# A recommender kernel: SyncE fetches the rows of 7 of its 416 gathers one by one, and rows are buffered for four tiles

## What is computed

```python
e = jnp.stack([tbl_0[ids[:, 0]], ..., tbl_25[ids[:, 25]]], axis=1)
x = layer_norm(dense_t @ Wd.T, gd, bd)
y = layer_norm(jnp.einsum('bnd,ed->bne', sparse_t, Ws), gs, bs)
y = layer_norm(jnp.einsum('bne,pn->bep', y, Wsi), gsi, bsi)
T = jnp.concatenate([x[:, None, :], jnp.swapaxes(y, 1, 2)], axis=1)
Z = jnp.einsum('bnd,bmd->bnm', T, T)
out = layer_norm(Z[:, TRIL_I, TRIL_J] @ Wl.T, gl, bl) * mask
h = jnp.maximum(jnp.concatenate([z, r_dense_t], axis=1) @ W_top1 + b_top1, 0.0)
h = jnp.maximum(h @ W_top2 + b_top2, 0.0)
y = h @ W_top3
```

## Time and profile before

| what | value |
|---|---|
| median of 3 runs | 592.68 us (590.53 to 594.43) |
| the profiled execution | 590.05 us |
| its span, first to last instruction | 588.3 us |
| mean granted TensorE clock | 0.962 |
| busy PE, PEld, DVE, ACT, POOL | 87%, 67%, 68%, 48%, 69% |
| instructions | 17016 |

### The profile page before, as it was taken

How to read it: one execution, slowest core, us unless ns; L and a number is a source line. 1 busy time by engine, 2 the same in 40 slices (tenths; PEclk the granted TensorE clock), 3 DMA queues, 4 the chain that set the end, 5 groups by cost and what they waited for, 6 DMA issues and landing times.

```text
span 588.3 us, 17016 instructions
## 1 busy us (share of the span) xinstructions
PE 511.5 (87%) x6783; PEld 396.6 (67%) x6783; DVE 402.2 (68%) x707; ACT 283.7 (48%) x727; POOL 406.5 (69%) x421
## 2 busy tenths in 40 slices
PE   2768768999999999999999988898899888998785
PEld 1654447678777777878787667676677666676564
DVE  2746766887878787787877766777577766777500
ACT  0513553545555464646464545454364545454422
POOL 6777777777777777777777777777777777773000
PEclk9958887999999999999999999999899999999999
DMA  7711113131313131313131312213131312212010
GB/s 266 270 27 28 25 29 87 27 89 28 88 29 87 30 88 28 90 29 87 29 91 26 88 28 67 50 36 81 28 88 28 88 28 66 50 30 75 2 62 2
DMA packets 27198, 36.39 MB, mean 62 GB/s; under 512 B 8917, under 2 KB 17775, under 8 KB 26607
## 3 DMA queue, kind: packets, MB, share of 16 engines
q0 software_dynamic: 13312, 13.66, 12.8%
q1 hardware_dynamic: 13808, 21.65, 10.9%
HBM read 26.09 MB, written 9.18 MB: 60 GB/s over the span
## 4 chain that ended last, share of the span: by engine, by line
PE 30%; DVE 22%; issue 16%; POOL 16%; ACT 8%; DMA 7%; SPq 1%; DVEq 0%; ACTq 0%
POOL rows L512 16%; PE bank_z L634 8%; DVE y L391 4%; PE bank_z L671 4%; DVE y_var L401 4%; DMA rows<-in_table,ids_all 4%; DVE r_vec L416 4%; PE bank_z L621 3%; PE bank_b L608 3%; PE bank_a L598 3%; DVE scaled L356 2%; ACT y_sq L761 2%; PE bank_z L587 2%; DVE y_r L408 2%; DMA wsi_b<-in_wsi_b 2%
## 5 line engine op out<-in xcount | busy, mean ns | idle before, releaser
L512 POOL DMA_INDIRECT rows<-in_table,ids_all x416 | 405.3, 974 | 126.8 <-issue 121.9
L401 DVE TENSOR_REDUCE y_var<-y_sq 128x32 f32<-128x1024 f32 x64 | 78.1, 1220 | 45.3 <-ACT y_sq L761 45.3
L761 ACT ACTIVATE y_sq<-y 128x512 f32<-128x512 f32 x128 | 80.4, 631 | 38.4 <-DVE y L391 38.0
L621 PEld LDWEIGHTS bank_z<-r_vec 128*32 128x32 f32 x4096 | 47.8, 112 | 60.6 <-issue 59.2
L608 PE MATMUL bank_b<-mixed,gs_row 64*128 64x512 f32 x128 | 74.7, 664 | 15.6 <-ACT mixed L790 15.4
L598 PE MATMUL bank_a<-wsi_b,scaled 128*128 128x192 f32 (+3 forms) x512 | 84.5, 309 | 2.1 <-DVE scaled L381 2.0
L416 DVE TENSOR_TENSOR r_vec<-y,y_r 128x512 f32<-128x512 f32 x128 | 82.9, 689 | 2.2
L598 PEld LDWEIGHTS bank_a<-wsi_b,scaled 128*128 128x128 f32 x512 | 78.5, 196 | 3.6 <-DVE scaled L381 3.2
L634 PE MATMUL bank_z<-wl,zd 128*128 128x512 f32 x160 | 77.7, 616 | 0.6 <-DMA zd<-zx 0.6
L608 PE MATMUL bank_c<-mixed,gs_row 64*128 64x512 f32 x128 | 74.7, 664 | 0.0
L783 ACT ACTIVATE row_std<-row_var,eps 128x8 f32<-128x8 f32 (+1 forms) x64 | 19.2, 300 | 103.8 <-DVE row_var L365 74.5
(11 more groups left out here) (99 smaller groups left out, 624.5 us busy)
## 6 DMA issues: line engine op xcount, KB each, us to landing
zx<-zs SPq DMA_DIRECT2D x16, 560.0 KB, 3.6
rows<-in_table,ids_all POOLq DMA_INDIRECT x416
dense_t<-in_dense_t SPq DMA_DIRECT2D x1, 2048.0 KB, 8.5
wl<-in_wl SPq DMA_DIRECT2D x1, 1280.0 KB
w<-in_w SPq DMA_DIRECT2D x1, 1280.0 KB, 16.2
zd<-zx SPq DMA_DIRECT2D x16, 80.0 KB
wsi_b<-in_wsi_b SPq DMA_DIRECT2D x1, 1248.0 KB, 11.6
zd<-zx SPq DMA_DIRECT2D x16, 70.0 KB
```

Of the source, the lines that this page charges most:

```text
L401: v.tensor_reduce(y_var[:, k % BANKS, :], y_sq[:, k % 2, :, :].rearrange("e a (s p) -> e (a s) p", p=PROJ), AX_X, ALU.add).then_inc(y_var_ ...
L512: nc.gpsimd.indirect_dma_start(rows[t % 2][:, c, D * blk:D * (blk + 1)], None, io["table"], bass.IndirectOffsetOnAxis(ap=ids_all[:, n:n + ...
L621: mm = pe.matmul(bank_i[PROJ * s:PROJ * (s + 1), n * ITEMS:(n + 1) * ITEMS], own[:, Y0:PAD], own, start=True, stop=True)
L761: nc.scalar.activation(y_sq[:, k % 2, blk, :], y[:, k % 2, blk, :], ACT.Square).then_inc(y_squared, 1)
```

## The change

One half of one chunk (chunk 12, half 1: the last gather of a tile) is no longer gathered by POOL in seven tiles: 1, 4, 6, 8, 11, 13 and 15. SP fetches those 7 x 128 rows instead. The ids of these rows are loaded as two small tensors (`sp_ids`, `sp_base`), added on DVE, and read by SP into registers, eight at a time (`TENSOR_LOAD`). For each row SP then computes the address from a register (listed as `ISA` below) and issues one DMA of one row into one partition of `rows`. The first 128 rows (tile 1) are fetched after the loads; after that each pass of SP's loop fetches 56 rows: 8 between the `zx` DMA and the wait for it, and 48 after the seven `zd` DMAs. Loop 13 has 40 rows left, loops 14 and 15 none. `rows` has four buffers instead of two, used in turn by tile, with semaphores to match; before the first row of a tile from 4 on, SP waits until the rows of the tile four before are scaled. PE waits, in the last quarter of these seven tiles, also for SP's 128 rows.

```diff
+SP_CHUNK, SP_BLK = CHUNKS - 1, 1
+SP_TILES = [1, 4, 6, 8, 11, 13, 15]
+SP_BATCH = 8
+SP_EARLY = 1
+SP_SHARE = 56
+BUFFERS = 4
...
+def by_sp(t, c, blk):
+    return t in SP_TILES and (c, blk) == (SP_CHUNK, SP_BLK)
+
+
+def gather_count(t, q):
+
+    return sum(not by_sp(i, c, blk) for i in range(t % BUFFERS, t + 1, BUFFERS) for c in GROUPS[q] for blk in range(2))
...
-        rows = [sb(f"rows{i}", [P, CHUNKS, 2 * D]) for i in range(2)]
+        rows = [sb(f"rows{i}", [P, CHUNKS, 2 * D]) for i in range(BUFFERS)]
...
             step(v.memset(ones[:], 1.0), "constants")
+            dve.wait_ge(sp_ids_loaded, 32)
+            v.tensor_tensor(sp_ids[:], sp_ids[:], sp_base[:], ALU.add).then_inc(sp_ids_ready, 1)
...
             for dst, src in ((ids_all, "ids"), (row_base, "row_base")):
                 sp.dma_start(dst[:], io[src]).then_inc(s_ids, 16)
+            for dst, src in ((sp_ids, "sp_ids"), (sp_base, "sp_base")):
+                sp.dma_start(dst[:], io[src]).then_inc(sp_ids_loaded, 16)
...
+            def fetch(first, end):
+
+                for at in range(first, end, SP_BATCH):
+                    u, p0 = divmod(at, P)
+                    t = SP_TILES[u]
+                    if p0 == 0 and t >= BUFFERS:
+                        sp.wait_ge(rows_scaled, BANKS * (t - BUFFERS + 1))
+                    _, found = nc.values_load_multi_w_load_instructions(
+                        sp_ids[u:u + 1, p0:p0 + SP_BATCH], engines=(mybir.EngineType.SP,), min_val=0,
+                        max_val=io["table"].shape[0] - 1, skip_runtime_bounds_check_because="ids are rows of the tables")
+                    for n, row in enumerate(found):
+                        p = p0 + n
+                        sp.dma_start(rows[t % BUFFERS][p:p + 1, SP_CHUNK, D * SP_BLK:D * (SP_BLK + 1)],
+                                     io["table"][bass.ds(row, 1), :]).then_inc(sp_rows[u], 16)
+
+            sp.wait_ge(sp_ids_ready, 1)
+            fetch(0, SP_EARLY * P)
             sp.wait_ge(prep, prep_at["zd"])
             for t in range(TILES):
...
                 sp.dma_start(zx.rearrange("j p k g i -> (j p) k g i"), zs[:]).then_inc(z_out, 16)
+                done = [min(SP_EARLY * P + n, len(SP_TILES) * P)
+                        for n in (SP_SHARE * t, SP_SHARE * t + SP_BATCH, SP_SHARE * (t + 1))]
+                fetch(done[0], done[1])
                 sp.wait_ge(z_out, Z_OUT * (t + 1))
...
+                fetch(done[1], done[2])
...
-                if t >= 2:
-                    pool.wait_ge(rows_scaled, k - 2 * BANKS + 1)
+                if t >= BUFFERS:
+                    pool.wait_ge(rows_scaled, k - BUFFERS * BANKS + 1)
                 for c in GROUPS[q]:
                     for blk in range(2):
+                        if by_sp(t, c, blk):
+                            continue
...
-                pe.wait_ge(gathered[t % 2][q], (t // 2 + 1) * (32 * len(GROUPS[q])))
+                pe.wait_ge(gathered[t % BUFFERS][q], 16 * gather_count(t, q))
+                if t in SP_TILES and q == BANKS - 1:
+                    pe.wait_ge(sp_rows[SP_TILES.index(t)], 16 * P)
```

More of the change, by code:

```diff
@@ L115, in tower @@
         row_base = sb("row_base", [P, 2 * CHUNKS], I32)
+        sp_ids = sb("sp_ids", [len(SP_TILES), P], I32)
+        sp_base = sb("sp_base", [len(SP_TILES), P], I32)
         ws_t = sb("ws_t", [P, E])
@@ L178, in tower @@
             sem(n) for n in ("ids_loaded", "small_loaded", "wsi_loaded", "wl_loaded", "dense_loaded", "top_loaded"))
-        gathered = [[sem(f"gathered_{parity}_{g}") for g in range(len(GROUPS))] for parity in ("even", "odd")]
+        gathered = [[sem(f"gathered_{n}_{g}") for g in range(len(GROUPS))] for n in range(BUFFERS)]
+        sp_rows = [sem(f"sp_rows_{t}") for t in SP_TILES]
+        sp_ids_loaded, sp_ids_ready = sem("sp_ids_loaded"), sem("sp_ids_ready")
         ids_ready = sem("ids_ready")
@@ L356, in square_form @@
                 v.tensor_tensor(scaled[:, a:b, :], bank_g[:, 0:(b - a) * P].rearrange("p (c n) -> p c n", n=P),
-                                rows[t % 2][:, a:b, :], ALU.mult).then_inc(quad_done, 1)
+                                rows[t % BUFFERS][:, a:b, :], ALU.mult).then_inc(quad_done, 1)
             def row_mean_square(k):
@@ L381, in scale_rows @@
                 v.tensor_tensor(scaled[:, a:b, :].rearrange("p c (a d) -> p (c a) d", d=D),
-                                rows[t % 2][:, a:b, :].rearrange("p c (a d) -> p (c a) d", d=D),
+                                rows[t % BUFFERS][:, a:b, :].rearrange("p c (a d) -> p (c a) d", d=D),
                                 row_r[:, 2 * a:2 * b].rearrange("p (n o) -> p n o", o=1)
@@ L506, in gather @@
                 t, q = divmod(k, BANKS)
-                if t >= 2:
-                    pool.wait_ge(rows_scaled, k - 2 * BANKS + 1)
+                if t >= BUFFERS:
+                    pool.wait_ge(rows_scaled, k - BUFFERS * BANKS + 1)
                 for c in GROUPS[q]:
                     for blk in range(2):
+                        if by_sp(t, c, blk):
+                            continue
                         n = t * 2 * CHUNKS + 2 * c + blk
                         nc.gpsimd.indirect_dma_start(
-                            rows[t % 2][:, c, D * blk:D * (blk + 1)], None, io["table"],
-                            bass.IndirectOffsetOnAxis(ap=ids_all[:, n:n + 1], axis=0)).then_inc(gathered[t % 2][q], 16)
+                            rows[t % BUFFERS][:, c, D * blk:D * (blk + 1)], None, io["table"],
+                            bass.IndirectOffsetOnAxis(ap=ids_all[:, n:n + 1], axis=0)).then_inc(gathered[t % BUFFERS][q], 16)
             for k in range(QUARTERS):
@@ L580, in turn @@
                 for n, c in enumerate(GROUPS[q]):
-                    mm = pe.transpose(bank_t[:, n * P:(n + 1) * P], rows[t % 2][:, c, :], ident[:])
+                    mm = pe.transpose(bank_t[:, n * P:(n + 1) * P], rows[t % BUFFERS][:, c, :], ident[:])
                 mm.then_inc(turned, 1)
@@ L965, in laid_out @@
         "row_base": np.repeat(first_row[feature].T, 2, axis=1).astype(np.int32),
+        "sp_ids": ids[:, SP_TILES, SP_CHUNK, SP_BLK].T,
+        "sp_base": np.broadcast_to(first_row[feature[SP_CHUNK]].astype(np.int32), (len(SP_TILES), P)),
         "ident": np.eye(P, dtype=f32),
```

## The result

The changed kernel takes **606.46 us** (median of 4 runs, 604.08 to 608.00) against 592.47 us of the kernel before on the same chip (4 runs): a ratio of 1.0225, with a 95% interval of 1.0194 to 1.0255. It is slower by 14 us where 9 us less was forecast. The profiled execution has a span of 605.0 us, the one before 588.3.

What follows compares the result with a forecast made beforehand. The prediction took GpSimd's gathers as the bound, SyncE having room for the rows at 29.6 us a loop; seven gathers fewer gave 592.68 - 8.95 = 583.7 us, with a range of 579 to 612.

Steps and rivals of the forecast that it cites:

- its own first rival: SyncE's queue: batches over 4.10 us make SyncE the bound; 612 us at 4.4; nearly all of 0.26.
- What bounds the kernel, and what the removal is worth: GpSimd's gathers set the pace, compute having 21 us to give; seven fewer gathers save 8.95 us.
- 7 x 1.278 = 8.95 us: GpSimd: seven gathers removed at 1.278 us each, all of it on the path that sets the end.
- Four buffers therefore gain nothing by themselves: GpSimd's buffer waits: two buffers were enough, so four gain 0 and only let SyncE fetch early.
- The gathers get slower: Rival, GpSimd's gathers: single rows double the hiccups, 596 us, or half that, 590; ending within 1% shares 0.17.
- A batch is then 8 x 0.40 + 0.55 = 3.75 us: SyncE: eight rows at 0.40 us plus one register load at 0.55; bounds 2.8 and 7.3 us.
- zx of loop 14 must start by 527.3: SyncE's last loop that waits for fetches: the limit, leaving 4.10 us a batch; forecast start 493, 34 us to spare.
- PE stop at L634 for zd: PE's linear layer: under the first rival, late zx and zd stop PE here, as it runs in order.
- The price per 0.1 us of a batch, 9.6 us: SyncE: from 4.10 us a batch, each 0.1 us more delays the end by 96 x 0.1 = 9.6 us.
- a margin of only 0.11 us per row: SyncE's row cost: a point for the first rival, beside a limit of 0.51 us a row.
- issue time falls with the number of partitions: SyncE's DMA issue: a point against the first rival, 0.43 us at 128 partitions to 0.25 at one.
- 0.57: Chance given to the forecast: all of the 9 us, or enough to be faster by over 1%, below 586.8 us.

Runs made afterwards that it cites:

- the removal alone: The kernel before with seven gathers left out and nothing in their place: 583.5 us against 592.06, ratio 0.985.
- two zs tiles: The changed kernel with two zs buffers in place of one: 604.89 us, ratio 1.0205 to the kernel before.

## Why the prediction was wrong

The forecast took the wrong side of its own first rival, to which it gave nearly all of 0.26: SyncE became the bound.

- *What bounds the kernel, and what the removal is worth: right.* "7 x 1.278 = 8.95 us" and 583.7 us; the removal alone gives 583.5.
- *"Four buffers therefore gain nothing by themselves": right*, ratio 0.9995.
- *"The gathers get slower": did not happen.* 980 ns with and without SyncE's rows. The changed kernel's gathers ended at 530.1, not at 527.7, but so did those of the removal alone (start of the last at 529.0).
- *"A batch is then 8 x 0.40 + 0.55 = 3.75 us": the step that failed, a mis-sized term.* The row was nearly right (0.41 for 0.40). The load was not: 0.78 and its gap for 0.55, taken from the middle of a range of 0 to 1.1 for want of a row. With the dearer loads behind zx and the batches of 4.5 us the mean is 4.23, 0.48 more, 3.4 us in a loop of seven.
- *"zx of loop 14 must start by 527.3": the second step that failed, a limit set at the wrong loop.* SyncE had issued its last row before loop 14 at 540.45, 13 us past that limit, and still waited 4.8 us for `zs`. What held the end was loop 13: its zx left at 516.03, and ACT's copy of the next tile's first quarter had to wait for it until 520.76, and with ACT all that stands behind that copy; the stages of tile 14 that follow take their own time whatever SyncE does. In the removal alone, where SyncE waits in every loop, zx of loop 13 leaves at 489.26, so here it is 26.8 us late; the span is 22.6 us longer (605.0 against 582.4). Part of such lateness is made up behind loop 13: with loads of 24 ids that zx is 10.7 us late (499.92), and the span only 1.3 us longer (583.7). I had credited loop 13's shorter stretch of rows, which lies behind that point. I also had PE stop at L634 for zd; ACT's copy stands earlier, and PE stops there only when ACT no longer does (two zs tiles).
- *The price per 0.1 us of a batch, 9.6 us: right in size, a little low.* The profiled executions with loops of 31.7 us and 32.9 us took 585.46 and 606.76: 21.3 us for 1.2 us of loop, 12 for each 0.1 us of a batch. With 583.5 as the floor the cost sets in near 31.6 us a loop, a batch of 4.0; this is an estimate from these two points. The prediction had 3.3 + 7 x 4.10 = 32.0. With 4.23 its rival would have given 596; the measured 606.5 is 10 us more, the limit being set too late and the price too low.
- *"a margin of only 0.11 us per row": a wrong reading.* The 0.51 us a row from which it was taken holds the load too. Without it the margin was (4.10 - 3.75) / 8 = 0.04 us a row.
- *"issue time falls with the number of partitions": not even in the rows of before.* The zx DMA with 128 partitions took 0.34 us to issue, and the second zd DMA, with 28, took 0.41 (at 303.17). The row DMA came out at 0.225 all the same.

The chain at the end of the changed kernel, answering to the earlier trace rows:

```profile
515.71 0.23 SPq L515
...
516.03 4.66 DMA zx<-zs
...
520.76 0.04 ACT zs L848
...
529.11 3.13 PE bank_z L685 x6
```

The last row of loop 12 goes out at 515.71, zx of loop 13 right behind it, ACT's copy when zx has landed, and L685 follows in PE's order, without a wait for zd; the gathers, over by 530.1, stand nowhere in it. The linear layer of tile 14 stood at 543.70 before, and stands at 559.25 now: 15.6 of the 16.7 us that the span has grown.

What I should have seen: the margin of the forecast was 4.10 - 3.75 = 0.35 us a batch, and the bounds of the one unseen instruction alone were 1.1 us wide. With a cost that is paid 112 times on the engine that feeds everybody, the middle of such a range is no basis for a forecast; 0.57 was too much for it.

## What to carry to other kernels

Work given to an engine that waits most of the time has to fit into its loop, to the tenth of a microsecond: here 48 rows a loop gain 7 us, 56 lose 14. When such an engine also carries a transfer that others wait for, its lateness adds up from loop to loop (1.2 us more a loop cost 21 us here), and a second buffer at one of the waits only moved the wait to the next user. Before moving work, count the small instructions around the one that is wanted: dropping the address arithmetic (0.08 us a row) was enough to turn the change into the gain it was meant to be.

## What the runs showed of the hardware

- A load of registers from SBUF on SyncE took 0.783 us for 8 ids, 1.227 for 16 and 1.669 for 24: 0.34 us and 0.055 us per id.
- A DMA of one row with its address in a register took 0.225 us to issue, less than the 0.25 of the one-partition store with a fixed address; the two register instructions ahead of it took 0.037 and 0.029 us, but with the gaps around them a row came every 0.41 us, and every 0.33 us without the multiplication.
- 896 one-row DMAs beside the gathers left these at 980 ns a piece, as without them.
- With SyncE as the bound the mean granted clock of PE was 0.938 over the span, against 0.962 before and 0.965 with the removal alone; PE was busy 86% of the span, 87% before. Up to zx of loop 13 the loops go by SyncE's queue, which waits for no other engine but once for 0.6 us, so PE's clock can cost little there. Behind it the clock was 0.88 from 516.0 to 545.3, and 0.95 from the last zx to the end, 31.3 us; with the removal alone that last stretch took 29.2 us at 1.00. What share of the loss goes back to the clock was not tried.
